# A decoder kernel's expert loop: both transposes of a step put ahead of its gate/up and down

## The reference, cut to what matters

```python
scores = jax.nn.sigmoid(x @ gate_w)
_, selected_experts = jax.lax.top_k(masked_scores, K)      # K = 6, from 2 of 4 groups
weights = weights / jnp.sum(weights, axis=-1, keepdims=True)
xs = x_exp[sort_idx]                                       # rows sorted by expert
g = jax.lax.ragged_dot(xs, w_gate, group_sizes)            # 256 -> 176
u = jax.lax.ragged_dot(xs, w_up, group_sizes)              # 256 -> 176
d = jax.lax.ragged_dot(jax.nn.silu(g) * u, w_down, group_sizes)   # 176 -> 256
expert_out = jnp.sum(out * weights[..., None], axis=1)
```

## Time and profile before

| | us |
|---|---|
| median of three runs | 929.71 |
| lowest, highest | 925.07, 933.79 |
| profiled execution, its time | 931.42 |
| its span in the profile | 929.6 |
| PE busy in the span | 768.7 (83%) |
| DVE, ACT, POOL busy | 478.0, 304.3, 213.0 |

### The profile page before, as it was taken

The page is one execution under the profiler, slowest core; times in us unless marked ns, Lnnn a source line. Parts: engine busy times, 40 slices in busy tenths (PEclk is TensorE's granted clock), DMA queues, the critical chain, the costliest instruction groups (busy, mean ns, idle before and its releaser), DMA issues. The chain is left out here.

```text
span 929.6 us, 18265 instructions
## 1 busy us (share of the span) xinstructions
PE 768.7 (83%) x6887; PEld 470.8 (51%) x6887; DVE 478.0 (51%) x1239; ACT 304.3 (33%) x703; POOL 213.0 (23%) x267
## 2 busy tenths in 40 slices
PE   4599988777839996999999999869969999999900
PEld 4467765555514443555556666647734444444400
DVE  6745665666326883445545444425943333333337
ACT  0012333444221000133333333323335555555500
POOL 3200121111000001000000000023436666666510
PEclk9999998999658995699999999977989999999965
DMA  9492000000020000000000000019312222222263
GB/s 302 125 291 67 2 3 2 2 3 2 1 91 0 1 0 1 1 1 1 2 2 1 2 1 2 1 46 257 118 40 86 86 86 86 86 87 88 71 218 116
DMA packets 48123, 55.28 MB, mean 59 GB/s; under 512 B 7366, under 2 KB 43174, under 8 KB 47334
## 3 DMA queue, kind: packets, MB, share of 16 engines
q1 hardware_dynamic: 38246, 34.11, 12.4%
q0 software_dynamic: 6656, 16.85, 5.4%
q10 hardware_dynamic: 3136, 3.15, 1.0%
HBM read 41.45 MB, written 12.65 MB: 58 GB/s over the span
## 5 line engine op out<-in xcount | busy, mean ns | idle before, releaser
L609 DVE TENSOR_REDUCE nmf<-bank 128x4 f32<-128x512 f32 x192 | 123.7, 686 | 138.8 <-PE bank L295 138.6
L495 ACT ACTIVATE pt<-bank 128x512 f32<-128x512 f32 x192 | 104.2, 595 | 252.3 <-PE bank L315 252.3
L295 PE MATMUL bank<-kk,qT 32*128 32x256 f32 x768 | 115.5, 419 | 15.2 <-ACT pt L495 8.3
L726 POOL TENSOR_TENSOR rstd<-vare,half 128x1 f32<-128x1 f32 x32 | 17.7, 552 | 438.8 <-DVE vare L670 438.8
L295 PEld LDWEIGHTS bank<-kk,qT 32*128 32x128 f32 x768 | 70.7, 194 | 53.6 <-issue 36.8
L1464 PE MATMUL bank<-wgu,g_xgT 128*64 x256 | 90.6, 477 | 0.0
L1464 PE MATMUL bank<-g_wgu,g_xgT 128*64 128x352 f32 x256 | 90.6, 477 | 0.0
L315 PE MATMUL bank<-nm,sel 32*128 32x128 f32 x768 | 86.4, 343 | 0.0
L307 PE MATMUL bank<-qT,kk 32*128 32x512 f32 x256 | 78.0, 687 | 1.7 <-ACT pt L495 1.4
L1429 POOL DMA_INDIRECT out_rows<-g_og,g_out_row x64 | 63.4, 990 | 58.1 <-DVE g_og L1533 54.9
L1484 PE MATMUL bank<-wd,g_hT 128*64 x256 | 68.9, 392 | 0.1
(11 more groups left out here) (243 smaller groups left out, 1370.5 us busy)
## 6 DMA issues: line engine op xcount, KB each, us to landing
wgu<-in_L_ffn_w_gate SPq DMA_DIRECT2D x4, 1408.0 KB
wgu<-in_L_ffn_w_up SPq DMA_DIRECT2D x4, 1408.0 KB
wd<-in_L_ffn_w_down SPq DMA_DIRECT2D x32, 176.0 KB
g_y<-out_rows SPq DMA_DIRECT2D x4, 768.0 KB, 16.6
g_y<-out_rows ACTq DMA_DIRECT2D x4, 768.0 KB, 17.2
sparse_table<-f_m_re SPq DMA_DIRECT2D x2, 1024.0 KB
f_m_re<-sparse_table SPq DMA_DIRECT2D x2, 1024.0 KB
f_idx_row<-in_L_ffn_mask_idx SPq DMA_DIRECT2D x1, 1024.0 KB
```

The lines of the kernel that those rows point to most:

```text
L295: return pe.matmul(bank, q, k, start=first, stop=r == 1, skip_group_check=True)
L495: act.activation(T.pt[2 * (t % 2) + u][:, :], STB[u][:, :], ACT.Exp, scale=own[v].scale).then_inc(exp_done, 1)
L609: dve.tensor_reduce(T.nmf[v % 2][:, 2 * (c % 2) + u, at:at + 4], SB[u][:, :].rearrange("p (h k) -> p h k", h=4), AX.X, ALU.max, negate=Tru ...
```

## The change

In TensorE's step the h transposes of slot c go up, right behind the x transposes of slot c + 2; gate/up of c + 1 follows, and then down, which is now of slot c instead of c - 1. The other engines follow. ScalarE's step becomes: load of the expert number of slot c + 2, x copy of c + 2, hT copy of c, weight copy of c + 2 (before: of c + 3), silu of c + 1. VectorE's step becomes: h of c + 1, output copy of c (before: of c - 1), copy of down weights of c + 2 (before: of c + 1). GpSimd's step becomes: gather of c + 5, scatter of c (before: of c - 1). Buffers, tiles and instructions stay the same. The diff, whole:

```diff
--- before.py
+++ after.py
@@ -1423,7 +1423,7 @@
                         pool.wait_ge(xt_done, n - 3)
                     pool.indirect_dma_start(G.xg[n % 4][:], None, G.x_rows[:, :],
                                             bass.IndirectOffsetOnAxis(ap=G.x_row[:, n:n + 1], axis=0)).then_inc(gathered[n % 4], 16)
-                n = c - 1
+                n = c
                 if has(n):
                     pool.wait_ge(out_ready, n + 1)
                     pool.indirect_dma_start(G.out_rows[:, :], bass.IndirectOffsetOnAxis(ap=G.out_row[:, n:n + 1], axis=0),
@@ -1452,6 +1452,14 @@
                     for j in range(KT):
                         last = pe.transpose(trx[n % 2][:, j * 128:(j + 1) * 128], G.xg[n % 4][:, j * 128:(j + 1) * 128], T.ident[:])
                     last.then_inc(xt_done, 1)
+                n = c
+                if has(n):
+                    pe.wait_ge(h_ready, n + 1)
+                    if n >= 2:
+                        pe.wait_ge(ht_ready, n - 1)
+                    for j in range(2):
+                        last = pe.transpose(trh[n % 2][0:MH, j * 128:(j + 1) * 128], G.h[n % 2][:, j * MH:(j + 1) * MH], T.ident[:])
+                    last.then_inc(tr_done, 1)
                 n = c + 1
                 if has(n):
                     pe.wait_ge(xt_copied, n + 1)
@@ -1466,14 +1474,6 @@
                     last.then_inc(gu_done, 1)
                 n = c
                 if has(n):
-                    pe.wait_ge(h_ready, n + 1)
-                    if n >= 2:
-                        pe.wait_ge(ht_ready, n - 1)
-                    for j in range(2):
-                        last = pe.transpose(trh[n % 2][0:MH, j * 128:(j + 1) * 128], G.h[n % 2][:, j * MH:(j + 1) * MH], T.ident[:])
-                    last.then_inc(tr_done, 1)
-                n = c - 1
-                if has(n):
                     pe.wait_ge(ht_ready, n + 1)
                     if n >= 2:
                         pe.wait_ge(out_ready, n - 1)
@@ -1497,22 +1497,22 @@
             def step(c):
                 n = c + 2
                 if has(n):
+                    unit = act.value_load(G.unit[0:1, SHARE * n + 1:SHARE * n + 2], min_val=0, max_val=UNITS - 1)
                     act.wait_ge(xt_done, n + 1)
                     act.activation(G.xgT[n % 2][:], trx[n % 2][:, 0:D], ACT.Copy).then_inc(xt_copied, 1)
+                n = c
+                if has(n):
+                    act.wait_ge(tr_done, n + 1)
+                    act.activation(G.hT[n % 2][0:MH, :], trh[n % 2][0:MH, 0:256], ACT.Copy).then_inc(ht_ready, 1)
+                n = c + 2
+                if has(n):
+                    if n >= 2:
+                        act.wait_ge(gu_done, n - 1)
+                    act.activation(G.wgu[n % 2][:], T.wgu[:, bass.ds(unit, 1), :, :].rearrange("p a k n -> p (a k) n"), ACT.Copy).then_inc(wgu_ready, 1)
                 n = c + 1
                 if has(n):
                     act.wait_ge(gu_done, n + 1)
                     act.activation(G.sil[n % 2][:], gu[n % 2][:, 0:MI], ACT.Silu).then_inc(sil_ready, 1)
-                n = c
-                if has(n):
-                    act.wait_ge(tr_done, n + 1)
-                    act.activation(G.hT[n % 2][0:MH, :], trh[n % 2][0:MH, 0:256], ACT.Copy).then_inc(ht_ready, 1)
-                n = c + 3
-                if has(n):
-                    if n >= 2:
-                        act.wait_ge(gu_done, n - 1)
-                    unit = act.value_load(G.unit[0:1, SHARE * n + 1:SHARE * n + 2], min_val=0, max_val=UNITS - 1)
-                    act.activation(G.wgu[n % 2][:], T.wgu[:, bass.ds(unit, 1), :, :].rearrange("p a k n -> p (a k) n"), ACT.Copy).then_inc(wgu_ready, 1)
 
             act.wait_ge(T.low_loaded, T.low_count)
             act.wait_ge(T.high_loaded, T.high_count)
@@ -1525,13 +1525,13 @@
                 if has(n):
                     dve.wait_ge(sil_ready, n + 1)
                     dve.tensor_tensor(G.h[n % 2][:], gu[n % 2][:, MI:2 * MI], G.sil[n % 2][:], ALU.mult).then_inc(h_ready, 1)
-                n = c - 1
+                n = c
                 if has(n):
                     dve.wait_ge(down_done, n + 1)
                     if n >= 4:
                         dve.wait_ge(scattered[n % 4], landed(n, 1))
                     dve.tensor_copy(G.og[n % 4][:], down_bank[n % 2][:, 0:D]).then_inc(out_ready, 1)
-                n = c + 1
+                n = c + 2
                 if has(n):
                     if n >= 2:
                         dve.wait_ge(down_done, n - 1)
```

## The result

| | before | after |
|---|---|---|
| median on the same chip, us (4 runs each) | 927.39 | 936.95 |
| lowest, highest | 923.92, 933.79 | 933.23, 939.06 |
| profiled execution, its span | 931.42, 929.6 | 935.85, 934.1 |
| x transposes of step 2 and of step 61 | 696.17, 877.11 | 692.96, 882.55 |
| mean step between them (59 steps) | 3.067 | 3.213 |

The ratio is 1.0083 [1.0043, 1.0123]: slower by 0.8%. The forecast was 912.6, with a range of 906 to 922. The experts stage tells the loss: 59 x (3.213 - 3.067) = 8.6 us of the 9.6.

A forecast was written before the change was run, and what follows sets the result against it. TensorE's full instruction row was taken to bound the experts stage; its step falls from 3.067 to 2.775 us (2.745 plus 0.03 for waits), saving 17.1 us with the ends: 929.71 - 17.1 = 912.6 us, range 906 to 922.

The forecast's parts named there:

- TensorE's order: TensorE's experts step: two of four passages between matmuls and transposes vanish, giving 2.745 us, 0.32 less than now.
- the near bound that I chose: Last gate/up to first down on TensorE: a plain round, 0.295 us, rather than 0.40 + 0.055.
- Does the data come in time?: Experts step: silu and h ready before the h transposes, slack 0.26 us; waits cost 0.03, giving period 2.775.
- silu starts 0.51 behind the last round: ScalarE's silu begins 0.51 us after the start of TensorE's last gate/up round, read from before's trace.
- The 0.03 us of the release: Term in the chain from silu to the h transposes: a release between engines costs 0.03 us.
- GpSimd's queue: GpSimd's gather and scatter take 2.26 us per step, still leaving some 0.5 us waiting at 2.775; cost nothing.
- The ends: Start and end of the experts stage, timed around sixty steps of 2.775 us; saved in all 17.1 us.
- The rule on the clock: Transposes don't hold TensorE's clock up; a 0.88 us piece between matmul rounds might lower it (rival chance 0.02).
- C: Rival: ScalarE's register load on the path by the copies delays silu; period 3.19, 7.6 us slower, 937; chance 0.04.
- A: Rival: the chain through h sets the step, 2.75 to 2.9 us; 920 at a period of 2.9; chance 0.18.
- D: Rival: weight loads hidden in all TensorE passages, last down to T at 0.215 too; period 2.65, 907; chance 0.04.

The follow-up runs named there:

- e_no_gather: Changed kernel with only the first four gathers issued, their rows used again for all slots; 916.95 us (1 run), mean step 2.785 us.
- e_no_scatter: Changed kernel with all 64 scatters issued behind the loop; 1002.26 us (1 run, 82 us of it those scatters), mean step 2.784 us.
- e_silu_first: Changed kernel with ScalarE's silu moved ahead of the weight copy; 949.01 us, ratio 1.0114 to before.
- e_alternate: Changed kernel with every second gather left out from slot 4 on; 922.24 us, ratio 0.9943 to before.
- e_lag3: Changed kernel with h transposes one slot later, down two, copies and scatter shifted too, giving every wait about a step; 932.20 us, ratio 1.0061 to before.

## Why the prediction was wrong

Step by step, in its own order:

- *TensorE's order* was right to a hundredth or two per term; `e_no_gather` and `e_no_scatter` have the step of 2.78 that was forecast as 2.775. Gate/up to down took 0.29, the near bound that I chose.
- *Does the data come in time?* Silu, h, the h transposes in time: all right as long as TensorE's reports are. **The step that failed is "silu starts 0.51 behind the last round"**, the term that holds TensorE's report of gate/up. It was read from one step and taken as fixed, with a slack of 0.26 us behind it. In the long steps of after silu starts 1.5 us behind or more, 1.57 in the step shown: over 1.0 us late, so h is late and TensorE idle ahead of the h transposes (0.61 us at 773.91). The 0.03 us of the release behind silu held: 773.49 to 773.51. Before could have carried a late silu: there h had a whole gate/up of time.
- *GpSimd's queue* was the other half of the same error: "Cost nothing; with the cover gone the period would be 2.26, no bound". Its pause, 0.80 us, went to 0.49. I asked whether GpSimd would be in time for others, and never what goes with its transfers when the pause shrinks.
- *The ends*: at the start nearly as forecast. The stage begins 4.3 us earlier in this profile (first x transposes at 682.18 for 686.51) and T of step 2 comes 3.2 earlier, so the start lost 1.1 us where 0.9 was forecast. What failed lies between: 59 steps took 8.6 us more instead of 17.2 less.
- *The rule on the clock*: the granted clock stayed 1.00 in this stretch, with pieces of 0.32 + 0.58 us between matmul rounds. Of the Trainium skill's rule on transposes, "TensorE: Matmul & The Clock Gate", Part 4: PE-mode transpose, nothing was to be seen.
- *The rivals*: C named the time, 937, and the place, a silu that is late; but its mechanism, the register load on the path by the copies to silu, is not it (`e_silu_first`), so the time was luck. A named the idle time ahead of the h transposes, and gave it tenths. None of them let the cause come from outside the chain that I had drawn. D's sum has a slip that changes nothing here: a period of 2.65 gives 905, and its 907 belongs to 2.68.

What is shown: the late reports come with gathers and scatters together and go when either is left out; they are no matter of ScalarE's order, TensorE's register loads, or the bytes of a gather; at 2.78 us the three added waits, meant to move the issues within the step, did not help; before's own order has them as soon as its step is 0.22 us shorter, or its pause is put elsewhere. What stays open: by which path GpSimd's transfers hold up TensorE's reports and no one else's, whether the two kinds or their number and spacing count, and why before's order escapes at 3.07 us while the new one does not even at 3.22. Every time here is of an execution that the profiler recorded, so whether the recording takes part in the delay is not shown either.

None of these kernels is an advance on before with all the work in it. Those that beat it leave out a quarter of the transfers or nearly half (`e_alternate`, and `e_no_gather` in one run). By these runs GpSimd would need fewer indirect transfers for the same rows to make the new order pay; that was not found.

## What to carry to other kernels

A pause in an engine off the critical path is not free slack: in before's order 0.80 us of idle GpSimd in each step went together with TensorE's signals on time, and 0.49 us in the changed order with signals 1 us and more late. Before a change shortens a step, look in the trace of before for places where such a pause already happens to be short, and see what the other engines do there. When consumers of one producer start late, out of idle time and 0.04 us apart, suspect its signals before its work.

## What the hardware showed that was not expected

- TensorE's completion signals can be over 4 us late while it works on (743.80 to 748.82 in `e_lag3`); ScalarE's and VectorE's were on time beside late ones (773.49 to 773.51 in after).
- Late signals come out 0.04 us apart (774.64 and 774.68), and once, with several held, TensorE itself stopped between two transposes until they came (748.79 in `e_lag3`).
- An indirect gather of 128 rows keeps GpSimd 0.97 us whether a row is 256 or 128 numbers long.
- Taking out 0.22 us of TensorE work per step made a kernel 0.7% slower (1.0066 [1.0025, 1.0107]).
